# Products for attention's maxima that name 64 of the 128 rows of the TensorE array

## The chip, the cores and the metric

The kernel runs on one core of one Trainium2 chip. Its time is the device time of an execution in microseconds; the number to predict is the median of the runs.

## The reference, cut to what matters

Two layers over x, which holds 4 sequences of 1024 rows of 256 numbers. The change lies in the second layer's cross-attention, which has 16 heads of 16 numbers each and a context of 154 rows for each sequence:

```
q = query.reshape(N, Q, 16, 16);  k = key.reshape(N, K, 16, 16);  v likewise
energy = einsum('nqhd,nkhd->nhqk', q, k)
energy = where(mask == 0, -1e20, energy)
attn = softmax(energy / sqrt(256), axis=-1)
out = einsum('nhqk,nkhd->nqhd', attn, v).reshape(N, Q, 256)
x = x + out @ W_out.T
```

A first layer with a projection and eight experts stands ahead of it, and a quantized feed-forward stage behind it.

## The kernel before, in words

Attention takes the 4096 rows of x in eight blocks of 512 (s = 0 to 7), each of four tiles of 128 rows (k), and the heads in four groups of four (g). A softmax needs the maximum of its row first. The kernel gets it from cheap products in bf16 (L1448) and then computes the real scores in four-byte numbers (L1482, and L1486 for the last 26 context rows), into which the maximum goes as one more row of the operands.

For the maxima, `qTb` holds the queries of a group with 32 partitions for each of its four heads (16 numbers, a one for the mask, zeros). `Kb` holds the keys in the same partitions, one strip of 154 columns for each head (4 strips side by side, [128, 4 groups, 4 heads, 154]). The function `maximum(s, m)` multiplies one tile of one group, with m = 4 g + k: a pair of matmuls of 308 columns, one for heads 0 and 1 and one for heads 2 and 3, into the two banks of a pair of PSUM banks. In `Kb`'s first two strips only partitions 0 to 63 are not zero, and in its last two only 64 to 127. Then VectorE reduces the 4 x 154 columns to four maxima (L1179), and the pair of banks comes free.

The order of the work on each engine is written out by hand. Within a block there are 20 steps. In every step `attention_tensor` issues the score of the next step, at steps 0, 5, 10 and 15 the four products for the values (L1502, each with 32 columns of the array), one step later the product with the last context rows (L1505, full array), three steps later the transposes back (L1513), and then what a table lists for the step, where "m" is `maximum` for the next block, "q" the transposes of the queries (L1463), "b" the transposes in bf16 (L1428), "a" those of the result (L1523) and "w", "W" the two halves of the projection (L1542):

```
LATER_PE = ("mm", "m", "m", "m", "mm", "mm", "m", "am", "", "wWm", "qm", "q", "", "qm", "", "m", "m", "", "b", "q")
```

Blocks 1 to 6 use this table; block 0 has one of its own, with its own maxima as well as those of block 1, and four of them stand ahead of the loop with filling matmuls between them (`kept_running`, L1601). "m", "q", "b", "a" and "w" share two pairs of banks in turn (`TURN`, `claimed`). ScalarE turns the scores into exponentials (L1305), with two banks for the scores, and copies transposed operands to SBUF (L1331, L1320).

In the feed-forward stage, L2092 multiplies one row of ones by one row of maxima (one row of the array), and L2108 are filling matmuls of the full array behind it.

Of the kernel before, what the change touches and what calls it, by code (L numbers as in the profile page):

```python
# [24 lines left out]
S2 = 154  # L25
# [193 lines left out]
def build(nc, a, out):  # L219
    with ExitStack() as ctx:  # L220
# [3 lines left out]
        def sb(stack, name, shape, dt=F32):  # L224
            return stack.enter_context(nc.sbuf_tensor(name, shape, dt))
# [31 lines left out]
        PR, G, GH, MW, SW = HEADS // 2, 4, 4, 32, 64  # L257
# [439 lines left out]
        h = flat[:, 6 * WE:6 * WE + HC * CAP].rearrange("p (c t) -> p c t", c=HC)  # L697
# [262 lines left out]
        with ExitStack() as st:  # L960
# [17 lines left out]
            QN = QT * P  # L978
# [21 lines left out]
            qTb = sb(st, "qTb", [P, QT, G, P], BF16)  # L1000
            Kb = [Kb0, sb(st, "Kb1", [P, G, GH, S2], BF16)]
# [61 lines left out]
            def wait_done(eng, *use):  # L1063
                i, n = TURN[use]
                eng.wait_ge(done[i], n + 1)
# [346 lines left out]
            def attention_tensor(pe):  # L1412
                def claimed(*use):

                    i, n = TURN[use]
                    pe.wait_ge(done[i], n)
                    return pair[i], full[i]
# [14 lines left out]
                def maximum(s, m):  # L1432
                    if s >= NQ:
                        return
                    dst, sent = claimed("mx", s, m)
                    g, k = m // QT, m % QT
                    if s == 0 and m < 2:
                        if m == 0:
                            pe.wait_ge(q_part, 1)
                        else:  # L1440
                            wait_done(pe, "tb", s, 0)
                    elif m == 0:
                        wait_done(pe, "tb", s, 0)
                    if m == 0:
                        if s % 2 == 0:
                            pe.wait_ge(k_kb, (s // 2 + 1) * NKB)
                    for u in range(2):
                        mm = pe.matmul(dst[:, u * QN:u * QN + 2 * S2], qTb[:, k, g, :],  # L1448
                                       Kb[s // 2 % 2][:, g, u * 2:u * 2 + 2, :].rearrange("p h s -> p (h s)"), start=True, stop=True)
                    mm.then_inc(sent, 1)  # L1450

                def turn(s, f):
# [105 lines left out]
                for i in range(2):  # L1558
                    for c in range(DC):
                        for n in range(HIC):  # L1560
                            w = wn[:, i * HIC * D + n * D + c * P:i * HIC * D + n * D + (c + 1) * P]
                            mm = pe.transpose(bank[i * DC + c][:, n * P:(n + 1) * P], w, ident)
                        mm.then_inc(f_wt, 1)
                pe.wait_ge(f_cp, 2 * DC)
                for g in range(2):
                    for c in range(3):
                        for n in range(DC):
                            at = 2 * HIC * D + n * HI + (g * 3 + c) * P
                            mm = pe.transpose(bank[g][:, c * D + n * P:c * D + (n + 1) * P], wn[:, at:at + P], ident)
# [4 lines left out]
                def filler(kind, s):  # L1574
                    if kind == "xt":
                        count[kind] = count.get(kind, -1) + 1
                        if count[kind] == NQ - 1:
                            pe.wait_ge(p_done, NQ * UNITS)
                            pe.wait_ge(u_wh, 1)
                            for _ in range(16):  # L1580
                                pe.matmul(bank[2][:, 0:QN], uwh[:, 0:P], uwh[:, 0:QN], start=True, stop=True)
                        normal_turn(count[kind])
                    if not 0 <= s < NQ:
                        return
                    i = count[kind, s] = count.get((kind, s), -1) + 1
                    if kind == "tb":
                        turn_bf16(s)
                    if kind == "mx":
                        maximum(s, i)
                    if kind == "qt":  # L1590
                        turn(s, i)
                    if kind == "at":
                        features(s)
                    if kind == "wo":
                        project(s, 0)
                    if kind == "wo2":
                        project(s, 1)
# [838 lines left out]
```

## Time and profile before

| | |
|---|---|
| median of 3 runs | 815.07 us (814.76 to 815.62) |
| span of the profiled execution | 814.1 us |
| instructions | 11786 |
| PE busy | 690.2 us, 85% |
| VectorE busy | 632.6 us, 78% |
| ScalarE busy | 486.0 us, 60% |
| GpSimd busy | 313.7 us, 39% |
| mean granted TensorE clock | 0.933 |

The span runs from the first to the last instruction of one profiled execution; the device time of the runs holds about a microsecond more. PE is the row of matmuls and PEld that of weight loads, which overlap matmuls. Matmuls are pipelined, so the recorded one starts before the one ahead of it has ended: what one occupies is seen in the distance from start to start.

### The profile page before, as it was taken

Reading aid. Unit: us, or ns where it says so; the run is one execution under the profiler, and the core shown is the slowest. Engines: PE = TensorE matmul, PEld = TensorE weight load, DVE = VectorE, ACT = ScalarE, POOL = GpSimd, SP = SyncE. Lnnn points to the kernel's source line nnn. Section 1 sums busy time; section 2 is a strip of 40 time slices with the busy share of each in tenths; the row PEclk is TensorE's granted clock in tenths of the full one; section 3 lists DMA queues with packets and bytes.
Section 4 is the critical chain, followed back from the end, with each engine's and each line's share of the span. In section 5 each row is a group of like instructions: output and inputs, shape, how many; then the busy total and the mean of one; then the engine's idle time right before and its main releaser. Section 6 shows DMA issues by size and latency. Waiting matters only on the chain.

```text
span 814.1 us, 11786 instructions
## 1 busy us (share of the span) xinstructions
PE 690.2 (85%) x4152; PEld 529.5 (65%) x4152; DVE 632.6 (78%) x1244; ACT 486.0 (60%) x621; POOL 313.7 (39%) x249
## 2 busy tenths in 40 slices
PE   6882029999999888999999999999999999009998
PEld 5761026899888754566566656577887888007998
DVE  5988894887777388887767675987888899997654
ACT  2223012554454437796896886666655999796873
POOL 4353604377677735234422420003440444693000
PEclk9995558999999999999999999999999999658999
DMA  9927523456644570010013000003310743201343
GB/s 299 339 81 257 200 80 110 127 137 146 178 88 58 108 254 1 1 47 27 1 47 130 1 27 27 27 27 133 127 52 1 261 152 131 76 0 53 125 135 104
DMA packets 59540, 84.95 MB, mean 104 GB/s; under 512 B 7904, under 2 KB 47712, under 8 KB 57952
## 3 DMA queue, kind: packets, MB, share of 16 engines
q1 hardware_dynamic: 49936, 61.09, 22.3%
q0 software_dynamic: 7872, 21.11, 10.5%
q10 hardware_dynamic: 1680, 2.08, 0.8%
q8 instruction: 30, 0.49, 0.3%
q14 instruction: 22, 0.18, 0.1%
HBM read 53.73 MB, written 30.54 MB: 104 GB/s over the span
## 4 chain that ended last, share of the span: by engine, by line
PE 63%; DVE 14%; ACT 7%; issue 4%; POOL 3%; DMA 1%; POOLq 0%; DVEq 0%; ACTq 0%
PE bank L2101 13%; PE bank L2363 11%; PE bank L2157 8%; PE bank L2387 5%; PE bank L1448 3%; PE bank L1482 3%; PE bank L1505 3%; PE bank L1542 3%; PE bank L1502 3%; DVE above L783 2%; PE bank L1463 2%; PE bank L1486 2%; ACT wgateT L2050 1%; DVE qx L1179 1%; ACT qT L1331 1%
## 5 line engine op out<-in xcount | busy, mean ns | idle before, releaser
L1305 ACT ACTIVATE x<-bank,bic 128x512 f32<-128x512 f32 x160 | 106.2, 697 | 34.1 <-PE bank L1482 32.6
L1179 DVE TENSOR_REDUCE qx<-bank 128x4 fp32r<-128x616 f32 x128 | 98.2, 796 | 27.0 <-PE bank L1448 25.6
L2101 PE MATMUL bank<-ux,uwh 128*128 128x512 f32 x384 | 96.6, 393 | 0.2 <-ACT ux L1995 0.2
L2101 PEld LDWEIGHTS bank<-ux,uwh 128*128 128x128 f32 x384 | 72.5, 189 | 16.0 <-issue 0.6
L1482 PE MATMUL bank<-qT,K 128*128 128x512 f32 x128 | 61.5, 490 | 3.5 <-ACT x L1305 2.0
L2324 ACT ACTIVATE wgateT<-bank 128x512 f32<-128x512 f32 x32 | 19.2, 599 | 65.7 <-PE bank L2363 65.7
L1448 PE MATMUL bank<-Kb,qTb 128*128 128x308 bf16 x256 | 53.2, 298 | 4.9 <-DVE qx L1179 2.2
L2101 PE MATMUL bank<-ux,uwl 128*128 128x512 f32 x192 | 52.0, 393 | 0.0
L1106 POOL CAST qx<-q 128x1024 fp32r<-128x1024 f32 x8 | 8.5, 1068 | 112.7 <-PE bank L1463 104.0
L2363 PE MATMUL bank<-xh,wh 128*128 128x512 f32 x128 | 50.0, 390 | 0.3 <-DVE xl L2297 0.3
L2363 PE MATMUL bank<-xl,wh 128*128 128x512 f32 x128 | 50.0, 390 | 0.0
L2363 PE MATMUL bank<-xh,wl 128*128 128x512 f32 x128 | 49.9, 390 | 0.0
L1448 PEld LDWEIGHTS bank<-Kb,qTb 128*128 128x128 bf16 x256 | 18.3, 97 | 46.3 <-DVE qx L1179 18.6
L2157 PE MATMUL bank<-uwh,oh 128*128 128x256 f32 x192 | 45.1, 277 | 0.5 <-DVE oh L1942 0.5
L2157 PE MATMUL bank<-uwl,oh 128*128 128x256 f32 x192 | 44.9, 276 | 0.0
L1331 ACT CAST qT<-bank 128x1024 fp32r<-128x1024 f32 x32 | 32.5, 1016 | 18.4 <-PE bank L1463 18.4
L2108 PE MATMUL bank<-uwh 128*128 128x512 f32 x39 | 12.0, 469 | 36.6 <-DVE peak L1834 36.6
L1121 POOL TENSOR_SCALAR q<-xr,mean,rstd 128x256 f32<-128x256 f32 x28 | 34.6, 1249 | 20.3 <-DVEq L1288 19.5
L2101 PEld LDWEIGHTS bank<-ux,uwl 128*128 128x128 f32 x192 | 36.6, 191 | 7.7
L707 POOL DMA_INDIRECT wupT<-row_dram,idx x16 | 16.5, 1030 | 56.7 <-DVE idx L869 28.0
L2157 PEld LDWEIGHTS bank<-uwh,oh 128*128 128x128 f32 x192 | 36.0, 188 | 1.0 <-DVE oh L1942 0.9
L2157 PEld LDWEIGHTS bank<-uwl,oh 128*128 128x128 f32 x192 | 36.1, 188 | 0.0
(420 smaller groups left out, 2029.0 us busy)
## 6 DMA issues: line engine op xcount, KB each, us to landing
xs_dram<-ux POOLq DMA_DIRECT2D x6, 1024.0 KB, 4.2
ux<-xs_dram POOLq DMA_DIRECT2D x6, 1024.0 KB, 5.3
x_dram<-x SPq DMA_DIRECT2D x4, 1024.0 KB, 5.5
xr<-in_w1T SPq DMA_DIRECT2D x8, 512.0 KB, 3.8
xr<-in_w3T SPq DMA_DIRECT2D x8, 512.0 KB, 4.7
xr<-in_w2T SPq DMA_DIRECT2D x8, 512.0 KB, 6.5
row_dram<-xn SPq DMA_DIRECT2D x8, 512.0 KB, 3.1
x_dram<-xr SPq DMA_DIRECT2D x8, 512.0 KB, 2.9
```

The lines of the kernel that those rows point to most:

```text
L1121: pool.tensor_scalar(q[:, k, :, :], xr[:, t, :].rearrange("p (h d) -> p h d", d=HD), mean[:, t:t + 1], rstd[:, t:t + 1], ALU.subtract, ALU ...
L1179: dve.tensor_reduce(qx[:, k, g * GH:(g + 1) * GH, MROW].rearrange("p (u h) -> p u h", u=2), pair[i][:].rearrange("p (u x) -> p u x", u=2)[ ...
L1305: act.activation(pr[g % 2][h], S_[u % 2], ACT.Exp, bias=bic[:, s // 2, h // GH:h // GH + 1]).then_inc(p_done, 1)
L1331: act.copy(qT[s % 2][:, 2 * f:2 * f + 2, :, :].rearrange("p n k t -> p (n k t)"), pair[i][:]).then_inc(done[i], 1)
L1448: mm = pe.matmul(dst[:, u * QN:u * QN + 2 * S2], qTb[:, k, g, :], Kb[s // 2 % 2][:, g, u * 2:u * 2 + 2, :].rearrange("p h s -> p (h s)"), ...
L1482: mm = pe.matmul(dst, K[b % 2][:, at // 2, at % 2, :], qT[s % 2][:, at // 2, :, :].rearrange("p k t -> p (k t)"), start=True, stop=True)
L1502: pe.matmul(O_[n % 2][j * 32:(j + 1) * 32, :], V[b % 2][:, g * GH + j, :], pr[n % 2][j], start=True, stop=False, skip_group_check=True)
L1505: pe.matmul(O_[n % 2], Vr[b % 2][:, g, :], pr[n % 2][j], start=False, stop=True, skip_group_check=True).then_inc(v_done, 1)
L2101: mm = pe.matmul(bank[j][:, m * TB:(m + 1) * TB], w[:, c * HI + cols:c * HI + cols + P], x[:, part, c * TB:(c + 1) * TB], start=(w is uwh ...
L2157: mm = pe.matmul(bank[i % 2][:, k * D:(k + 1) * D], o[t % 3][:, m * TB + k * P:m * TB + (k + 1) * P], w[:, c * D:(c + 1) * D], start=(o is ...
L2363: mm = pe.matmul(bank[1 + m][:, (c % 2) * CAP:(c % 2 + 1) * CAP], wp[i][:, m, d * H + c * P:d * H + (c + 1) * P], xp[i][:, d, :], start=(n ...
L2387: mm = pe.matmul(bank[3][:, k * D:(k + 1) * D], hp[:, c, k * P:(k + 1) * P], wp[i][:, 2, c * D:(c + 1) * D], start=(c == 0 and n == 0 and ...
```

## The change

Each product of a pair names the 64 partitions in which its heads lie, in both operands, instead of all 128.

```
@@ maximum
                     for u in range(2):
-                        mm = pe.matmul(dst[:, u * QN:u * QN + 2 * S2], qTb[:, k, g, :],
-                                       Kb[s // 2 % 2][:, g, u * 2:u * 2 + 2, :].rearrange("p h s -> p (h s)"), start=True, stop=True)
+                        rows = slice(u * 2 * MW, (u + 1) * 2 * MW)
+                        mm = pe.matmul(dst[:, u * QN:u * QN + 2 * S2], qTb[rows, k, g, :],
+                                       Kb[s // 2 % 2][rows, g, u * 2:u * 2 + 2, :].rearrange("p h s -> p (h s)"), start=True, stop=True)
                     mm.then_inc(sent, 1)
```

MW is 32. Scores, values, transposes and the waits are as before.

## Rows read from the trace of the kernel before

**Rows 1.** The page: busy shares and granted TensorE clock in 40 slices of the span.
```profile
PE   6882029999999888999999999999999999009998
PEclk9995558999999999999999999999999999658999
```

**Rows 2.** Lines of the maxima and of the values: count, ns (least/median/most), first and last start.
```profile
L1448 PE MATMUL bank<-Kb,qTb x256: 291/296/309, 290.0 to 506.0; 128*128 128x308 bf16 x128
...
L1502 PE MATMUL bank<-x,V x256: 589/593/617, 308.3 to 531.5; 128*32 128x512 f32 x128
```

**Rows 3.** Windows by round: length, busy time (count) per engine, clock, DMA.
```profile
core 0: us, PE busy (x) PEld busy (x) DVE busy (x) ACT busy (x) POOL busy (x), PEclk, DMA share, GB/s
290.00:303.00 13.00, 11.73 (x58) 7.01 (x57) 11.52 (x36) 4.13 (x5) 5.18 (x4) 1.00 0.90 308
303.00:334.19 31.19, 26.05 (x175) 14.88 (x176) 26.35 (x44) 21.02 (x28) 14.07 (x11) 1.00 0.00 1
334.19:363.13 28.94, 28.39 (x184) 17.33 (x182) 24.52 (x57) 25.23 (x37) 10.01 (x7) 1.00 0.10 26
391.95:420.77 28.82, 28.55 (x188) 17.72 (x186) 20.69 (x35) 25.21 (x38) 9.20 (x7) 1.00 0.10 32
420.77:449.59 28.82, 28.52 (x188) 17.73 (x186) 20.25 (x33) 21.94 (x32) 9.21 (x7) 1.00 0.28 94
```

**Rows 4.** The chain that ended last, through one round: shares by line; start, length, what.
```profile
by line: PE bank L1448 13.6%; PE bank L1482 13.3%; PE bank L1542 11.9%; PE bank L1505 11.8%; PE bank L1502 10.3%; PE bank L1486 8.1%; PE bank L1463 7.1%; issue 6.4%; ACT x L1305 4.4%; PE bank L1428 4.0%; ACT qT L1331 3.5%; PE bank L1523 3.0
...
394.66 1.02 ACT qT L1331
395.68 0.60 ACT x L1305
...
399.56 0.70 ACT x L1305
```

**Rows 5.** Timeline of PE's matmuls: start, length (of the merged run), what.
```profile
400.43 0.50 PE L1482 MATMUL bank<-qT,K 128*128 128x512 f32 x1
400.86 1.06 PE L1502 MATMUL bank<-x,V 128*32 128x512 f32 x8
401.86 0.70 PE L1448 MATMUL bank<-Kb,qTb 128*128 128x308 bf16 x4
402.29 0.49 PE L1482 MATMUL bank<-qT,K 128*128 128x512 f32 x1
402.63 1.02 PE L1505 MATMUL bank<-x,Vr 128*128 128x512 f32 x2
403.49 0.43 PE L1448 MATMUL bank<-Kb,qTb 128*128 128x308 bf16 x2
```

**Rows 6.** The same view ten microseconds later.
```profile
410.30 1.06 PE L1502 MATMUL bank<-x,V 128*32 128x512 f32 x8
411.29 0.88 PE L1463 MATMUL bank<-identr,qx 128*128 128x128 f32 x8
412.01 0.44 PE L1448 MATMUL bank<-Kb,qTb 128*128 128x308 bf16 x2
...
412.52 1.02 PE L1505 MATMUL bank<-x,Vr 128*128 128x512 f32 x2
413.27 0.90 PE L1463 MATMUL bank<-identr,qx 128*128 128x128 f32 x8
414.01 0.47 PE L1482 MATMUL bank<-qT,K 128*128 128x512 f32 x1
```

**Rows 7.** Timeline of PE's weight loads where one row of the array is named.
```profile
551.69 0.29 PEld L2092 LDWEIGHTS bank<-am,cst 1*128 1x128 f32 x2 [0.67 <-DVE am L1803]
552.00 0.30 PEld L2108 LDWEIGHTS bank<-uwh 128*128 128x128 f32 x2
```

**Rows 8.** The chain that ended last, in the first stretch of attention.
```profile
304.99 0.45 PE bank L1448 x2
305.46 1.52 DVE qx L1179 x2
```

## The prediction

> **What bounds the kernel now.** I read the page's slices first: TensorE's clock is granted in full through the attention stage, and PE is nearly always busy there [rows 1]. The products for the maxima (L1448) run only between 290.0 and 506.0 us; their line has 256 matmuls of 296 ns at the median, which is 128 pairs [rows 2]. The table of windows then splits this time by the rounds of the loop over s [rows 3]. From 334.19 us on, six rounds of about 28.82 us follow each other with PE busy for 28.5 of it, DVE for 20 to 25 and ACT for 22 to 25. Before 334 us it is different: 32 of the 128 pairs lie in 44 us in which DVE is nearly as busy as PE or busier. The chain of waits through one steady round says the same: it is PE's matmuls but for ACT steps of 1.02, 0.60 and 0.70 us and 6.4% of issue (about 1.8 us), so that some 24.7 of 28.8 us, 0.86 of the round, go by what PE takes [rows 4]. The stage after attention starts when attention ends, so time won or lost in the six rounds reaches the end of the kernel.
>
> **The change, part by part.** Nothing is added or moved: 256 matmuls and 256 weight loads stay, with the same 308 columns, banks, waits and semaphores. Each pair's two products now name rows 0 to 63 and 64 to 127 of the array. Two things can follow.
>
> *What it can save.* Today the second product of a pair starts about 0.13 us after the first: a pair takes 0.43 us where one takes 0.30, and four take 0.70 [rows 5]. That is 308 columns one after the other on one array. The four products for the values, which take 32 columns of the array each and so name disjoint parts of it, run side by side: eight matmuls of 0.59 to 0.62 us are over in 1.06 us, while two full ones of the same kind need 1.02 [rows 2, 5]. If the two halves of a pair do the same, the second starts some 0.01 us after the first and a pair saves 0.12 us. The Trainium skill ("TensorE: Matmul & The Clock Gate", Part 3) says that matmuls in different row groups run concurrently, about 4 ns apart; no row here shows it for rows, only the one above for columns.
>
> *What it can cost.* The products stand alone between matmuls that name all 128 rows, so if naming part of the array makes the engine empty itself on the way in and out, this is paid at every group of them. The values show such a price. Going in: a score followed by a full matmul starts it 0.34 us later (402.29 to 402.63), followed by the values 0.43 us later (400.43 to 400.86) [rows 5]: 0.09, say 0.10 us. Coming out to bf16 weights: 1.00 us from the values' start to the next product (400.86 to 401.86) against 0.86 for the same two passes at full width (402.63 to 403.49); 0.02 of the difference is four staggered starts, which leaves about 0.12, a little over the way in [rows 5]. Coming out to four-byte weights, whose load is longer and is not hidden any more: values, eight transposes and on to the next take 1.71 us (410.30 to 412.01), the full-width matmuls with eight transposes 1.49 (412.52 to 414.01) [rows 6]. The difference is 0.22, less 0.02 of stagger 0.20. The nearest row on rows of the array is L2092, which names one row: its two weight loads, which end within 0.29 us of 551.69 and take 0.18 each, start 0.11 apart, but the full matmul behind it, which waits for no semaphore, has its load start 0.20 after the second [rows 7]. Those 0.09 us of wait and about 0.10 for a load that is no longer ahead make 0.19. I take 0.10 in and 0.19 out, because what follows each group in the order written out is a score with four-byte weights. By what this trace shows that price is paid for columns, and by one case for one row; for 64 rows it is unknown: between nothing and 0.29.
>
> The Trainium skill ("TensorEngine Tiling (Array Packing)", Key Properties) has the rule that changing the tiling mode drains TensorE. Behind columns the trace agrees, with the 0.09 to 0.20 us above; if the rule holds for rows, the sum below is its result, and without it the sum would be that of the second rival.
>
> *The sum for a steady round.* LATER_PE holds 16 products in 13 groups. Nine are one pair between full matmuls: 0.10 + 0.19 - 0.12 = +0.17 each, +1.53. One is two pairs between full matmuls (behind turn_back): 0.29 - 0.24 = +0.05. Three stand directly behind the values, where the way out is paid already and becomes the way in: two of them with two pairs, 0.19 - 0.24 = -0.05 each, and one with one pair, 0.19 - 0.12 = +0.07. Together +1.55 us. Not all of it reaches the end: where PE waits for an exponential or for a bank, the emptying lies in the wait. With the 0.86 of above, +1.33 us a round, and +8.0 over six rounds.
>
> *The first 44 us.* Here DVE's reductions often follow a pair directly on the chain (0.44 us of L1448, then L1179) [rows 8], so that DVE would have its input 0.12 us sooner, while the emptying mostly lies in filling matmuls and waits. Thirty-two pairs at -0.12 with a third of them on the chain is -1.3; 14 or so single groups with +0.17 where PE is the one that is late is +2.4. I take +0.5, between -1 and +3.
>
> The profiled span is 814.1 us, 1.0 under the median of the runs (815.07); the sum of +8.5 is made on the span and carried over to the median: 823.6 us.
>
> **The rivals.** A, the forecast: side by side, and emptied at every change. With half the price hidden instead of a seventh it gives +4; with all of it on the path and 0.20 for each way in and out, 9 x 0.28 + 0.16 + 2 x -0.04 + 0.08 = 2.7 a round, +16. Its own range is 819 to 831. Chance 0.64.
>
> B, it wins: no emptying for halves of the rows, since four-byte and bf16 weights of full height follow each other without one and the columns may be a case apart. Then 0.12 x 16 x 0.86 = 1.65 a round, 9.9 over six, and a little more at the start, with half a microsecond lost again to ACT, whose 25.2 us in every other round is then not far from PE's 27: about 805.5 us. It decides if the price per group is under 0.15 us: 13 groups at 0.15 eat the 16 savings of 0.12. Against it stand the five readings of 0.09 to 0.20 above, none of which is on 64 rows. Chance 0.18.
>
> C, the change does nothing: the array takes 64 rows as a full-height matmul with the rest silent, without a change of mode. 308 columns pass one after the other, as now: 815.1. Chance 0.07.
>
> D, emptied at every change, but the halves one after the other, because the second one's weights wait for the first. Then 10 x 0.29 + 3 x 0.19 = 3.5 a round, 3.0 with the 0.86, +18 over six and +3 ahead of them: about 836 us. Chance 0.08.
>
> E, the granted clock falls in attention, because half the array is silent. It is full from 150 us to 600, also over stretches in which the values name a quarter each [rows 1], and it fell only where PE stood still for long. One round at the half clock would cost up to 25 us: 840. Chance 0.03.
>
> **How the numbers follow.** The time is A's, 823.6. The range takes A and C whole and the lower part of B that reaches 805: 0.64 + 0.07 + about 0.10, which leaves out the rest of B, D and E: 805 to 831. A measurement of this kernel can tell about 0.2% (1.6 us) from no change. Faster by more: B, 0.18. Within: C and a sliver of A that is hidden, 0.09. Slower: 0.73.
>
> **What would show it.** In the changed kernel L1448's forms read 64*128, and a pair takes about 0.31 us instead of 0.43 if the halves run side by side. If the engine empties itself, the matmul behind each group (L1482, L1486) starts some 0.3 us after the pair's second where it now starts 0.03 us after it, the weight loads of L1448 show issue before them behind a score, and the six rounds last about 30.1 us; by B they last about 27.2, by C 28.8, by D 31.8. The granted clock stays at full. Wrong would make it: an emptying that 64 rows don't cause, one that is larger than for columns, or more slack in PE's waits than a seventh of the round.

## The result and the profile after

The changed kernel takes 824.72 us (median of 4 runs, 823.69 to 825.71), the kernel before 814.99 in the runs beside it (4 runs, 814.76 to 815.62). The ratio is 1.0111, with a 95% interval of 1.0077 to 1.0144: slower by 9.7 us. The forecast was 823.6. The profiled execution has a span of 822.1 us, 8.0 more than before, and a mean granted clock of 0.929. It took 823.93 us, 1.8 more than its span, and in every later profile the two lie 1.75 to 1.86 us apart, not about one. By that the profiled execution of the kernel before took about 815.9 us (an estimate: its time is not on record), 0.9 above its median, where the changed kernel's is 0.8 below. So the profiles compare a rather long execution with a rather short one, and their 8.0 is less than the 9.7 of the medians.

The page's slices of busy time and clock, to be laid beside [rows 1]:

```profile
PE   6881039999999789999999999999999999009998
PEclk9996559999999997999999999999999999558999
```

PE stays as busy, and nothing changes after attention. New is a 7 in the clock's row, in a slice in which it was granted in full before. The line of the products (L1449 now) and its weight loads:

```profile
L1449 PEld LDWEIGHTS bank<-Kb,qTb x256: 92/92/102, 289.5 to 514.0; 64*128 64x128 bf16 x128
L1449 PE MATMUL bank<-Kb,qTb x256: 287/301/437, 289.5 to 514.0; 64*128 64x308 bf16 x128
```

The form is 64*128, as foreseen: the array is named by halves. One product still takes 0.30 us; what changed is how two of them stand to each other and to their neighbours. The timeline of PE in a steady round, at the place of [rows 5]:

```profile
402.55 0.50 PE L1483 MATMUL bank<-qT,K 128*128 128x512 f32 x1
402.98 0.30 PE L1449 MATMUL bank<-Kb,qTb 64*128 64x308 bf16 x2
403.21 0.74 PE L1487 MATMUL bank<-qT,Kr 128*128 128x512 f32 x2
403.89 0.30 PE L1449 MATMUL bank<-Kb,qTb 64*128 64x308 bf16 x2
404.12 0.50 PE L1483 MATMUL bank<-qT,K 128*128 128x512 f32 x1
404.46 0.60 PE L1514 MATMUL bank<-cst,x 128*128 128x128 f32 x4
404.99 0.44 PE L1449 MATMUL bank<-Kb,qTb 64*128 64x308 bf16 x4
405.35 0.51 PE L1483 MATMUL bank<-qT,K 128*128 128x512 f32 x1
405.79 1.07 PE L1503 MATMUL bank<-x,V 128*32 128x512 f32 x8
...
407.15 0.50 PE L1483 MATMUL bank<-qT,K 128*128 128x512 f32 x1
407.49 1.02 PE L1506 MATMUL bank<-x,Vr 128*128 128x512 f32 x2
408.44 0.30 PE L1449 MATMUL bank<-Kb,qTb 64*128 64x308 bf16 x2
408.68 0.50 PE L1483 MATMUL bank<-qT,K 128*128 128x512 f32 x1
```

Three distances are to be read. A pair takes 0.30 us in all, no more than one product, and four take 0.44 where they took 0.70: the halves run side by side. From L1506 (before: L1505) to the pair behind it are 0.95 us (407.49 to 408.44) where they were 0.86 (402.63 to 403.49) [rows 5]: 0.09 more on the way in. And the score behind a pair starts 0.24 us after it (408.44 to 408.68, 403.89 to 404.12, both with pairs that are one product long), where before it waited 0.43 - 0.30 = 0.13 us for the second product and 0.02 to 0.04 more (403.49 to 403.64, and from 401.86 to 402.29 are three further products and 0.04) [rows 5]. So a pair and its way out take 0.07 to 0.09 us more than before, and with the way in a single group takes 0.17 us more.

The weight loads (PEld) show what waits. The score's load, before and then after:

```profile
403.62 0.19 PEld L1482 LDWEIGHTS bank<-qT,K 128*128 128x128 f32 x1
```

```profile
408.68 0.19 PEld L1483 LDWEIGHTS bank<-qT,K 128*128 128x128 f32 x1
```

Before, it starts as the pair's second product does, 0.13 us after 403.49, and runs beside it. After, both products start at 408.44, and the load starts only 0.24 us later, close to their recorded end.

The windows of the two blocks ahead of the steady rounds and of one steady round, with the columns of [rows 3]:

```profile
287.27:312.54 25.27, 22.88 (x123) 12.02 (x124) 19.93 (x50) 10.74 (x14) 9.25 (x7) 0.93 0.56 189
312.54:337.15 24.61, 21.52 (x128) 11.08 (x127) 20.41 (x36) 15.23 (x21) 9.82 (x7) 0.86 0.00 1
...
396.64:426.29 29.65, 29.21 (x188) 16.84 (x186) 20.67 (x35) 25.57 (x38) 9.21 (x7) 1.00 0.10 32
```

The same two stretches of the kernel before. The first runs from the first bf16 transposes (L1428) to the next, the second from there to those ahead of the steady rounds:

```profile
287.93:311.42 23.49, 20.89 (x123) 12.32 (x124) 19.50 (x50) 10.56 (x14) 9.24 (x7) 1.00 0.59 202
311.42:334.04 22.62, 18.81 (x129) 10.94 (x127) 20.28 (x36) 15.35 (x21) 10.01 (x7) 1.00 0.00 1
```

A steady round is 29.65 us instead of 28.82 [rows 3], +0.83, and six of them are +5.0. The two blocks ahead are 49.88 instead of 46.11, +3.8, at a granted clock of 0.93 and 0.86. These add to +8.8, and attention began 0.7 earlier in this execution: +8.1, which is the 8.0 between the spans but for rounding.

### The profile page after: what moved, and what is told of

The parts are those of the page before. It is cut to its first block, busy times and chain, and to the rows that moved or that the text cites. A ratio compares the mean times of both kernels' runs of the same rounds, so it can differ in the third digit from the quotient of the medians.

```text
span 822.1 us, 11786 instructions
## 1 busy us (share of the span) xinstructions
PE 697.4 (85%) x4152; PEld 523.8 (64%) x4152; DVE 632.7 (77%) x1244; ACT 488.0 (59%) x621; POOL 314.1 (38%) x249
## 4 chain that ended last, share of the span: by engine, by line
PE 60%; DVE 13%; ACT 11%; issue 3%; POOL 3%; DMA 1%; POOLq 0%; ACTq 0%; DVEq 0%
PE bank L2364 11%; PE bank L2158 8%; PE bank L2102 7%; PE bank L1483 5%; PE bank L2388 5%; PE bank L1543 3%; PE bank L1506 3%; PE bank L1503 3%; PE bank L1449 3%; DVE above L783 2%; PE bank L1487 2%; PE bank L1464 2%; PE bank L1514 1%; ACT wgateT L2051 1%; DVE high L1884 1%
## 5 line engine op out<-in xcount | busy, mean ns | idle before, releaser
L1179 DVE TENSOR_REDUCE qx<-bank 128x4 fp32r<-128x616 f32 x128 | 98.6, 797 | 33.5 <-PE bank L1449 32.3
L1483 PE MATMUL bank<-qT,K 128*128 128x512 f32 x128 | 63.4, 505 | 4.7 <-ACT x L1305 4.2
L1449 PEld LDWEIGHTS bank<-Kb,qTb 64*128 64x128 bf16 x256 | 12.1, 93 | 51.3 <-issue 17.8
L1483 PEld LDWEIGHTS bank<-qT,K 128*128 128x128 f32 x128 | 23.9, 192 | 25.3 <-issue 10.1
L1449 PE MATMUL bank<-Kb,qTb 64*128 64x308 bf16 x256 | 36.6, 303 | 3.7 <-ACT qT L1331 1.6
```

The source lines that it names most:

```text
L1179: dve.tensor_reduce(qx[:, k, g * GH:(g + 1) * GH, MROW].rearrange("p (u h) -> p u h", u=2), pair[i][:].rearrange("p (u x) -> p u x", u=2)[ ...
L1449: mm = pe.matmul(dst[:, u * QN:u * QN + 2 * S2], qTb[rows, k, g, :], Kb[s // 2 % 2][rows, g, u * 2:u * 2 + 2, :].rearrange("p h s -> p (h ...
L1483: mm = pe.matmul(dst, K[b % 2][:, at // 2, at % 2, :], qT[s % 2][:, at // 2, :, :].rearrange("p k t -> p (k t)"), start=True, stop=True)
```

## The experiments

Times of a comparison are medians, beside runs of the kernel before on the same chip, whose median there was 815.8 to 816.4 us, with single runs from 813.2 to 819.3. Lengths of rounds come from the profiles, from L1428 to L1428, where the second and third steady round of every kernel agree to 0.04 us; the first is up to 0.2 us longer, and 0.9 in same_half and scores_too.

**Where the loss lies: the halves in the steady rounds alone, or ahead of them alone.**

```diff
-                        rows = slice(u * 2 * MW, (u + 1) * 2 * MW)
+                        rows = slice(u * 2 * MW, (u + 1) * 2 * MW) if s >= 2 else slice(0, P)   # late_only
+                        rows = slice(u * 2 * MW, (u + 1) * 2 * MW) if s < 2 else slice(0, P)    # early_only
```

> Halves only in the products for blocks 2 to 7, which stand in the six steady rounds; blocks 0 and 1, in the first 50 us of attention, name all rows as before. Mode theory (each change between naming all rows and naming half empties the array: 0.10 us in, 0.19 out, 0.12 saved per pair side by side, part of it absorbed in PE's waits for exponentials): the six rounds stay at 29.65 us, as in the changed kernel, so +5.0 us over before, 820.0, with the first stretch as in the kernel before. Rival (the loss is the 10 us at the half clock that the changed kernel's profile shows in its first stretch): rounds near 28.8, time within 1 us of before.

> Halves only in the products for blocks 0 and 1, all rows in the others. Mode theory: the rest of the loss, +3.1 to +3.8 us over before, 818 to 819, of which the switches are +2 or so and the rest the stretch at the half clock, if the profile shows one again; six rounds of 28.82 us. If the clock is what costs and it doesn't fall: nearer to +1.5. If late_only and early_only don't add up to the changed kernel's +9.7 within 2 us, they depend on each other.

late_only took 820.59 us against 816.01, ratio 1.0058 (1.0037 to 1.0079). Its steady round is as long as the changed kernel's:

```profile
364.24:393.92 29.68, 29.24 (x186) 16.88 (x185) 20.80 (x36) 22.32 (x32) 9.19 (x7) 1.00 0.09 27
```

early_only took 818.35 us against 816.01, ratio 1.0027 (1.0014 to 1.0041). Its windows are those of the changed kernel ahead of the steady rounds, and those of the kernel before in them:

```profile
288.14:313.37 25.23, 22.88 (x122) 12.12 (x123) 19.83 (x50) 10.72 (x14) 9.23 (x7) 0.93 0.55 188
313.37:338.27 24.90, 21.54 (x128) 10.88 (x127) 20.33 (x36) 15.23 (x21) 9.81 (x7) 0.86 0.00 1
...
367.25:396.07 28.82, 28.54 (x185) 17.74 (x185) 20.86 (x36) 21.96 (x32) 9.20 (x7) 1.00 0.09 29
```

The steady rounds lose their 0.83 us at full clock, so the clock can't be their cause. The two parts sum to 4.6 + 2.3 = 6.9 us, 2.8 short of the changed kernel's 9.7, more than the 2 us that I had allowed. It is not more than the intervals allow: they are 6.3 to 11.7 us for the changed kernel, 3.0 to 6.4 for late_only and 1.1 to 3.3 for early_only. Single runs of early_only range from 815.9 to 820.2, its profiled one being near the top with 820.2; those of the kernel before range as widely here, from 813.4 to 818.8. How much of the first stretch is the clock is asked further down.

**Are the halves side by side, and is it worth anything?** Both products name the same half. This leaves the maxima of heads 2 and 3 of each group out of the computation.

```diff
-                        rows = slice(u * 2 * MW, (u + 1) * 2 * MW)
+                        rows = slice(0, 2 * MW)
```

> Both products of a pair name rows 0 to 63 (the maxima of heads 2 and 3 of each group are then of other products, which leaves out part of the computation). Same changes of mode as in the changed kernel, but the two can't run side by side. Mode theory with side-by-side halves: the second product starts 0.13 us after the first, a single group costs 0.29 instead of 0.17, rounds of 31.3 to 31.8 us, in all 834 to 838 us. Rival (the halves never gained by being side by side, the recorded starts 3 ns apart are only issue): same time as the changed kernel, 824.7.

It took 834.91 us, ratio 1.0241 (1.0216 to 1.0267). Pairs take 0.43 us again, four take 0.70, and the way out is unchanged: the score starts 0.36 after the pair (413.02 to 413.38), which is 0.13 for the second product and 0.23.

```profile
413.02 0.43 PE L1449 MATMUL bank<-Kb,qTb 64*128 64x308 bf16 x2
413.38 0.50 PE L1483 MATMUL bank<-qT,K 128*128 128x512 f32 x1
```

Its rounds are 31.31 us, 1.66 more than the changed kernel's, where 16 pairs at 0.127 are 2.03. The halves of the changed kernel do run side by side, and without that the change would cost twice as much: 18.9 us here. This is what rival D had described.

**Is it the change between forms that costs?** One product of a pair by half, the other in full, so that a change stands within the pair and none behind it.

```diff
-                        rows = slice(u * 2 * MW, (u + 1) * 2 * MW)
+                        rows = slice(0, 2 * MW) if u == 0 else slice(0, P)
```

> The first product of a pair names rows 0 to 63, the second all 128. Nothing can run side by side; there is a change of mode in and one out within each pair, both to bf16 weights. Mode theory: +0.10 before the first and +0.10 between the two, nothing behind the second, 16 pairs at 0.20 is 3.2 us a round less what PE's waits take in (0.7 to 1.0), rounds near 31.1 us, in all about 833. Rival (the cost sits in leaving for four-byte weights alone): the matmul behind the pair starts 0.03 us after it as before, and the round is within 0.3 us of 28.8.

It took 831.27 us, ratio 1.0189 (1.0166 to 1.0213), with rounds of 30.71 us.

```profile
410.98 1.02 PE L1506 MATMUL bank<-x,Vr 128*128 128x512 f32 x2
411.93 0.54 PE L1449 MATMUL bank<-Kb,qTb 64*128 64x308 bf16 x2
412.20 0.50 PE L1483 MATMUL bank<-qT,K 128*128 128x512 f32 x1
```

The pair takes 0.54 us instead of 0.43: 0.10 to 0.11 between its products. The way in is 0.95 - 0.86 = 0.09 as in the changed kernel. Behind the second, a full product, the score comes at once (0.27 after the pair's start, of which 0.24 is the start of the second product). The price follows the change of form wherever it is put, and is not one of leaving for four-byte weights alone. Gross, that is before PE's waits take in a part, 16 pairs at 0.20 are 3.2 us, less 0.3 where the values stand ahead; 1.9 of it reach the round.

**Does it go by groups or by products?** The same 16 products of a steady round in 10 groups instead of 13, in full and by halves.

```diff
-            LATER_PE = ("mm", "m", "m", "m", "mm", "mm", "m", "am", "", "wWm", "qm", "q", "", "qm", "", "m", "m", "", "b", "q")
+            LATER_PE = ("mm", "", "mm", "", "mm", "mm", "mm", "am", "", "wWm", "qm", "q", "", "qm", "", "mm", "", "", "b", "q")
```

> The kernel before with the maxima of the steady rounds moved a step or so: 10 groups instead of 13 (mm at steps 0, 2, 4, 5, 6 and 15, single ones at 7, 9, 10, 13), the order of all other work unchanged. A control for grouped_half. All theories: within 3 us of before, since the same matmuls run in nearly the same order; it may lose a little where a second pair waits for VectorE.

> The changed kernel with the same regrouping. Mode theory: gross cost of the halves in a round 4 x 0.17 + 3 x 0.04 - 3 x 0.06 = +0.6 us instead of +1.5, so that the halves cost 6 x 0.4 or so less: +5 to +7 us against grouped_full instead of +9.7, of which some 4 in the first stretch, which isn't regrouped. Rival (cost per pair, not per group: reads or writes of halves are slower): the difference to grouped_full stays at 9 to 10 us.

The regrouping itself is dear: grouped_full took 823.14 us against 815.81, ratio 1.0094 (1.0076 to 1.0111), more than twice what I had allowed it. In its round of 29.87 us PE is busy for 28.86, so it stands still for a microsecond. 0.61 us of that lie ahead of the product at 378.68, which waits for VectorE to have reduced an earlier pair (L1179). grouped_half took 827.09 us, ratio 1.0149 (1.0124 to 1.0175). A round of each, full and then by halves:

```profile
366.18:396.05 29.87, 28.86 (x186) 17.77 (x185) 20.14 (x34) 22.01 (x32) 9.20 (x7) 1.00 0.08 27
```

```profile
366.03:396.34 30.31, 29.15 (x185) 16.59 (x185) 20.11 (x33) 22.12 (x32) 9.18 (x7) 1.00 0.08 27
```

By halves a round is 0.44 us longer than in full, where it was 0.83 longer in 13 groups. The difference of the medians is 3.95 us, under the 5 to 7 that I expected and far from the 9 to 10 of a price per product. By itself this doesn't settle the question, because the new waits for VectorE can take in a price as well. The starts around one group of two pairs do, in full and then by halves:

```profile
371.50 0.79 PE L1482 MATMUL bank<-qT,K 128*128 128x512 f32 x1
372.13 0.70 PE L1448 MATMUL bank<-Kb,qTb 128*128 128x308 bf16 x4
372.57 0.72 PE L1486 MATMUL bank<-qT,Kr 128*128 128x512 f32 x2
```

```profile
371.35 0.80 PE L1483 MATMUL bank<-qT,K 128*128 128x512 f32 x1
372.08 0.44 PE L1449 MATMUL bank<-Kb,qTb 64*128 64x308 bf16 x4
372.45 0.73 PE L1487 MATMUL bank<-qT,Kr 128*128 128x512 f32 x2
```

From the score ahead of the pairs to the product behind them are 1.07 us in full and 1.10 by halves. Two pairs together lose 0.03 us, where a pair alone loses 0.17: the price goes by groups.

**Halves where the way out is already paid.** Directly behind the values a change of form stands in the kernel before, too.

```diff
-                        rows = slice(u * 2 * MW, (u + 1) * 2 * MW)
+                        rows = slice(u * 2 * MW, (u + 1) * 2 * MW) if s >= 2 and m in (0, 1, 7, 8) else slice(0, P)
```

> Halves only for the four products a round (m = 0, 1, 7, 8, blocks 2 to 7) that stand directly behind the values, where the change of mode on the way out of the values is paid anyway; all rows elsewhere. Mode theory: 2 x (0.19 - 0.25) = -0.12 us a round before PE's waits, rounds of 28.7 to 28.82 us, the time equal to before within what can be told. Rival (halves cost per product): rounds 0.2 us longer, 29.0, since a quarter of the products is halved.

It took 815.53 us against 816.06, ratio 0.9992 (0.9979 to 1.0006), the same within what can be told. The rounds show the sign that the sum has there:

```profile
364.29:393.02 28.73, 28.29 (x185) 17.46 (x185) 20.80 (x36) 21.93 (x32) 9.20 (x7) 1.00 0.07 26
393.02:421.76 28.74, 28.31 (x186) 17.46 (x185) 20.67 (x36) 25.20 (x38) 9.20 (x7) 1.00 0.10 31
```

They are 0.08 us shorter than before, in rounds that differ by 0.02 among themselves; gross it should be 0.12. Only one of the two groups of two pairs can show it: from the pairs to the score the one at 374.33 takes 0.37 us, 0.06 less than in [rows 5], while at the other the score waits for ScalarE and comes 0.92 us after the pairs (367.89 to 368.81) with or without halves.

**Scores by halves as well.**

```diff
-                        mm = pe.matmul(dst, K[b % 2][:, at // 2, at % 2, :], qT[s % 2][:, at // 2, :, :]...
+                        rows = slice(at % 2 * SW, (at % 2 + 1) * SW)
+                        mm = pe.matmul(dst, K[b % 2][rows, at // 2, at % 2, :], qT[s % 2][rows, at // 2, :, :]...
```

> The changed kernel in which the scores (but not the product with the last 26 context rows) name their 64 rows as well. Mode theory: counted, the changes of mode in a steady round are 35 instead of 31 (8 before), because values, transposes and the last context rows still name all rows, but a score can run beside a product for the maxima or another score in the other half, so 820 to 828 us. Rival (naming half is dear only next to a score of full height, so halves throughout would be cheap): under 815 us.

It took 827.56 us, ratio 1.0148 (1.0123 to 1.0173), with rounds of 30.02 us: inside the first expectation, and far from the second. A score now follows a pair after 0.04 us (402.13 to 402.17), but matmuls of full height behind a score pay instead: the product with the last context rows starts 0.42 us after a score (406.48 to 406.90) where it was 0.34, as in the changed kernel (407.15 to 407.49). What the rest of the round adds is not shown.

```profile
402.13 0.30 PE L1449 MATMUL bank<-Kb,qTb 64*128 64x308 bf16 x2
402.17 0.49 PE L1484 MATMUL bank<-qT,K 64*128 64x512 f32 x1
```

**The clock in the first stretch.** 17 more filling matmuls in block 0, in the kernel before (full_warm) and in the changed one (half_warm), and the kernel before profiled once more as it is (full_again). From step 5 on the fillers write to the other bank of their pair.

```diff
-                WARM = {(1, 1): 3, (2, 0): 2, (2, 1): 4}
+                WARM = {(1, 1): 3, (2, 0): 2, (2, 1): 4, (2, 3): 2, (2, 4): 2, (3, 0): 2, (3, 1): 2, (4, 0): 1, (8, 0): 2, (8, 1): 2, (9, 0): 2, (9, 1): 2}
...
-                                kept_running(WARM[n, at], bank[3])
+                                kept_running(WARM[n, at], bank[3][:, QN:2 * QN] if n > 4 else bank[3])
```

> The kernel before, profiled once more, to see whether its own first stretch of attention ever loses the full clock. If halves alone make the clock fall, it stays full there and blocks take 46.1 us from the first bf16 transposes to those ahead of the steady rounds; if the stretch is at the edge anyway, it shows a fall in some executions, at 1.3 us or so for each 3.4 us at half clock.

> The kernel before with 17 more filling matmuls (0.23 us each) in block 0 of attention, where PE otherwise waits for VectorE. A control for half_warm: full clock through the stretch, and within 1 us of before, or a little less if before itself lost the clock in some executions.

> The changed kernel with the same 17 filling matmuls. If the first stretch's +4 us in the changed kernel's profile is the clock, the clock stays full, the stretch is within 0.5 us of full_warm's, and the whole difference to full_warm is that of the six rounds, +5.0 us, under the changed kernel's +9.7. If the stretch's loss is the changes of mode, the fillers change nothing: +9 us against full_warm.

The kernel before loses the clock there in some executions, too. Profiled again it took 816.23 us; its second block has a clock of 0.93 and is 1.20 us longer than in [rows 3]'s execution (23.82 against 22.62):

```profile
310.74:334.56 23.82, 20.26 (x128) 11.12 (x127) 20.36 (x36) 15.37 (x21) 10.02 (x7) 0.93 0.00 1
```

With the fillers the full rows take 815.93 us, ratio 0.9994 (0.9979 to 1.0008), and the halves 822.33, ratio 1.0084 (1.0061 to 1.0107): 6.4 us apart, where the changed kernel was 9.7 from the kernel before. The intervals of the two differences overlap; the windows show more. Full rows and then halves:

```profile
288.19:312.41 24.22, 22.53 (x131) 13.74 (x132) 19.73 (x50) 10.56 (x14) 9.24 (x7) 1.00 0.58 197
312.41:335.06 22.65, 20.43 (x137) 12.22 (x135) 20.29 (x36) 15.35 (x21) 10.04 (x7) 1.00 0.00 1
```

```profile
286.98:312.21 25.23, 24.05 (x131) 13.21 (x132) 20.19 (x50) 10.71 (x14) 9.23 (x7) 1.00 0.56 190
312.21:334.98 22.77, 20.74 (x136) 11.17 (x135) 20.41 (x36) 15.24 (x21) 9.86 (x7) 1.00 0.00 1
```

At full clock the halves cost 48.00 - 46.87 = 1.1 us in the first stretch, and 5.0 in the six rounds. That is 6.1 of the 6.4 us between the medians.

**Both small effects together.** behind_values with the fillers.

> Halves only directly behind the values in blocks 2 to 7, and the 17 filling matmuls in block 0. If both small effects add: rounds of 28.74 us instead of 28.82, full clock in the first stretch, 0.5 to 1 us under before, which five rounds may not tell from no change. Rival: the fillers cost in the first stretch what the clock gives back, and the time is that of before.

It took 816.36 us against 816.38, ratio 0.9999 (0.9983 to 1.0015). Its clock is full, and its rounds are 28.74 and 28.77 us, but block 0 is 0.7 us longer, as in full_warm. None of these kernels is faster than the kernel before by what can be told.

## Why the prediction was right

**The saving.** A pair by halves saves the second product's 0.13 us; I took 0.12. same_half, which takes only this away, costs 1.66 us a round more.

**The price of changing form.** 0.09 to 0.10 us on the way in, as taken from the values and expected at 0.10. The way out was taken as 0.19; in the rows it is 0.24 less 0.03 to 0.04, 0.20. A single group costs 0.17 us, as the sum had it. (The sign "some 0.3 us after the pair's second" was too long: by the prediction's own terms it is 0.03 + 0.19, and it measured 0.24.) That it is the change of form is shown by mixed, where it moves into the pair, by the starts in grouped_half, and by behind_values, where the halves save a little because no change is added. The rule of the Trainium skill ("TensorEngine Tiling (Array Packing)", Key Properties) is that changing the mode drains TensorE. For 64 rows the trace agrees, with these 0.09 to 0.20 us. Whether the array has to empty itself or only the weight load is held back, no run here tells apart. Rival B, which the rule spoke against, had the saving right and missed this price.

**What reaches the end: mis-sized.** The term "+1.55 us a round, times 0.86" measured 0.83, which is 0.54 of the gross. The share of PE on the chain says how much of a round is PE's time; it doesn't say how much slack (time in which PE would have waited anyway) stands right behind each lost piece. Of the 1.55, then, 0.72 went into such waits. From the score at 396.32, which waits for ScalarE in both kernels, up to the score at 400.43 in [rows 5] the round of before had three single groups and one of two pairs, 0.17 x 3 + 0.05 = 0.56 us gross. In the changed kernel that score starts at 405.35, and as the rounds begin 4.69 us apart (391.95 and 396.64) it is late by 0.23 only. The other 0.33 went where [rows 4] has a 0.70 us exponential at 399.56. The chain of the changed kernel has none there:

```profile
404.19 0.43 PE bank L1483
404.62 0.44 PE bank L1514 x4
405.06 0.37 PE bank L1449 x4
```

There PE came later and waited less for ScalarE. Another 0.17 went at the score that starts at 421.47 (before: 415.95). It is 0.83 us late, as the matmuls ahead of the single group before it already were (420.30 against 414.79, 0.82 late), because it waits for an exponential that is now on the chain:

```profile
420.63 0.70 ACT x L1305
```

The last 0.2 us went at the end of the round, where the product with the last context rows started 0.49 us behind its score before (419.55 to 420.04) and starts 0.34 behind it now (425.30 to 425.64).

**The first 44 us: mis-sized, with a cause that I had given to a rival.** I took +0.5, between -1 and +3; the profile has +3.8. Rival E, a fall of the clock, is the larger part of it: by the clock column of its windows (0.07 short of full over 25.27 us and 0.14 short over 24.61, twice that in time at 1.2 GHz, the half clock) the changed kernel ran 3.5 + 6.9, some 10 us of the stretch at half clock (an estimate). At full clock the stretch costs 1.1 us more by halves (half_warm against full_warm), within the bounds, so that by these profiles 2.7 of the 3.8 are the clock's. I had looked for E in the steady rounds, where it didn't come, and not ahead of them, where the kernel has filling matmuls and where even with full rows the clock is 0.93 in full_again. "The granted clock stays at full" was wrong there.

So the sum of +8.5 came out near the measured +9.7 partly by luck, because two errors met: the steady rounds gave 3.0 less than the 8.0 forecast, and the first stretch 3.3 more than the 0.5, most of that by the clock. With the clock kept full by fillers in both kernels, the halves cost 6.4.

**What stays open.** Whether halves make the clock fall more often. Of the five profiled executions with full rows and the old fillers ahead of the steady rounds, one kept the full clock there (before) and four had 0.93 in one block (full_again, late_only, behind_values, grouped_full). Of the six with halves there none kept it: the changed kernel and early_only had 0.93 and 0.86 in the two blocks, the other four between 0.86 and 0.93 in one. Two of those four (mixed and scores_too) had a 0.93 in one block, no lower than the kernels with full rows. That leans to yes, but each kernel was profiled once, the kernel before twice, and the two parts of the loss add up to no better than 2.8 us.

## What to carry to other kernels

Two halves side by side save one product's columns, 0.13 us here, but each change between part and whole has its price: 0.1 us on the way to a pair's bf16 weights, which load in 0.09 us, and 0.2 to four-byte weights of full height, which load in 0.19 and would otherwise load beside the product ahead. By these prices a pair alone loses, two pairs together about break even, and three would gain (0.29 against 0.38, an estimate; no run has three). Count the changes of form in the order of issue and not the matmuls, and put the partial ones next to others that are partial already, where they cost nothing (in behind_values the rounds were 0.08 us shorter and the time was the same). For what a lost piece does to the end, look at the first wait behind it, not at the engine's share of the chain.

## What the runs showed of the hardware that was not expected

The price is the same whether columns or rows are named: 128*32 and 64*128 matmuls both cost 0.09 us more on the way in, and going straight from one to the other costs the same as from 128*32 to full (1.00 us from L1503 to the pair behind it, 405.79 to 406.79, as in [rows 5]). And two 64*128 products of 308 columns take 0.30 us together, no more than one, although they write all 128 partitions of two different banks at once:

```profile
406.79 0.30 PE L1449 MATMUL bank<-Kb,qTb 64*128 64x308 bf16 x2
```
